# A GRU recurrence on one core: the columns of the first quarter of h are multiplied first, the rest behind them

## What is computed

```python
def cell(h, x):
    gi = x @ W_ih + b_ih
    gh = h @ W_hh + b_hh
    i_r, i_z, i_n = jnp.split(gi, 3, axis=-1)
    h_r, h_z, h_n = jnp.split(gh, 3, axis=-1)
    r = jax.nn.sigmoid(i_r + h_r)
    z = jax.nn.sigmoid(i_z + h_z)
    n = jnp.tanh(i_n + r * h_n)
    h_new = (1.0 - z) * n + z * h
    return (h_new, h_new)
xs = jnp.swapaxes(inputs, 0, 1)
_, hs = jax.lax.scan(cell, initial_state, xs)
```

## Time and profile before

| | us |
|---|---|
| median of 3 runs | 3862.88 (3861.38 to 3863.46) |
| the profiled execution | 3864.96 |
| its span in the trace | 3863.3 |
| TensorE busy in the span | 3556.0 (92%) |
| stretch 130 to 1815 us (nearly the whole recurrence): TensorE | 1616.2 of 1685.0, granted clock 1.00 |
| the same stretch: VectorE, ScalarE, GpSimd | 907.2, 851.8, 126.5 |
| the whole program: VectorE, ScalarE, GpSimd | 2105.9, 1586.6, 468.2 |

### The profile page before, as it was taken

How to read it: one execution, slowest core, us unless ns; L and a number is a source line. 1 busy time by engine, 2 the same in 40 slices (tenths; PEclk the granted TensorE clock), 3 DMA queues, 4 the chain that set the end, 5 groups by cost and what they waited for, 6 DMA issues and landing times. The chain is left out here.

```text
span 3863.3 us, 151423 instructions
## 1 busy us (share of the span) xinstructions
PE 3556.0 (92%) x60904; PEld 2248.5 (58%) x60935; DVE 2105.9 (55%) x6359; ACT 1586.6 (41%) x4769; POOL 468.2 (12%) x973
## 2 busy tenths in 40 slices
PE   5899999999999999998799999968899998999999
PEld 2578777888788878886444444424433333555554
DVE  2355555555555555554477777744466666532228
ACT  0255555555555555554344444422344444321110
POOL 1000000000000000000122222200000000024330
PEclk8999999999999999999999999979999998999999
DMA  4222222211111111111111111020111111259987
GB/s 140 87 78 77 71 71 78 66 27 25 28 26 24 27 30 27 27 27 33 57 58 38 38 57 38 19 80 22 50 57 57 57 57 40 76 177 308 295 249 295
DMA packets 220453, 298.87 MB, mean 77 GB/s; under 512 B 19955, under 2 KB 159503, under 8 KB 216416
## 3 DMA queue, kind: packets, MB, share of 16 engines
q1 hardware_dynamic: 201536, 244.94, 20.6%
q10 hardware_dynamic: 8032, 25.70, 2.3%
q0 software_dynamic: 10816, 27.33, 2.3%
HBM read 156.83 MB, written 63.96 MB: 57 GB/s over the span
## 5 line engine op out<-in xcount | busy, mean ns | idle before, releaser
L348 PE MATMUL gru_prz<-ahead,h 128*4 128x160 f32 (+1 forms) x32768 | 1179.8, 273 | 34.3 <-DVE h L459 15.1
L348 PEld LDWEIGHTS gru_prz<-ahead,h 128*4 128x4 f32 x32768 | 725.7, 87 | 201.2 <-DVE h L459 110.4
L348 PE MATMUL gru_pn<-ahead,h 128*32 128x128 f32 x16384 | 636.4, 273 | 3.5 <-issue 3.5
L348 PEld LDWEIGHTS gru_pn<-ahead,h 128*32 128x32 f32 x16384 | 509.6, 123 | 32.4 <-issue 3.8
L436 DVE STREAM_TRANSPOSE gru_tr<-gru_prz 128x160 f32<-128x160 f32 x512 | 179.0, 350 | 395.9 <-PE gru_prz L348 395.9
L410 ACT ACTIVATE gru_d<-gru_narg 128x8 f32<-128x8 f32 (+1 forms) x1024 | 209.8, 216 | 262.0 <-DVE gru_narg L447 262.0
L325 POOL COPY gru_rd<-giT 128x16 f32 x512 | 110.0, 215 | 1563.7 <-DVE h L459 1563.7
L440 DVE STREAM_TRANSPOSE gru_tn<-gru_pn 128x32 f32<-128x32 f32 (+1 forms) x1024 | 194.8, 228 | 161.2 <-PE gru_pn L348 161.2
L976 DVE TENSOR_REDUCE da_mx<-da_ps 128x2 f32<-128x1024 f32 (+3 forms) x256 | 201.1, 816 | 132.0 <-PE da_ps L669 132.0
L406 ACT ACTIVATE gru_rd<-gru_tr 128x20 f32<-128x20 f32 x512 | 122.1, 239 | 353.9 <-DVE gru_tr L436 353.9
L373 PE MATMUL gru_pgi<-gru_right,gru_left 128*128 128x128 f32 x960 | 233.8, 325 | 31.7 <-issue 29.3
(11 more groups left out here) (306 smaller groups left out, 4736.7 us busy)
## 6 DMA issues: line engine op xcount, KB each, us to landing
ahead<-in_L_ffn_gate_up_proj SPq DMA_DIRECT2D x64, 768.0 KB, 9.5
yk<-gru_zeros SPq DMA_DIRECT2D x29, 1024.0 KB, 5.0
ex_wd<-in_L_ffn_down_proj ACTq DMA_DIRECT2D x64, 384.0 KB, 8.1
ahead<-yk SPq DMA_DIRECT2D x16, 1536.0 KB, 9.6
gru_right<-ahead SPq DMA_DIRECT2D x60, 256.0 KB
gru_left<-ahead SPq DMA_DIRECT2D x60, 256.0 KB
ahead<-wide SPq DMA_DIRECT2D x15, 1024.0 KB, 4.7
ahead<-xnT SPq DMA_DIRECT2D x15, 1024.0 KB, 4.5
```

The costliest lines, as they stand in the source:

```text
L348: last = nc.tensor.matmul(rows(j), of(c), whh[:, c, j, cols], start=False, stop=True, skip_group_check=True)
```

## The change

- h's quarter 0 needs columns 0 to 31 of r, z and n. These are now multiplied first: r z0 is 64 columns (`RZ0`: r0, z0), n0 32 (`N0`), and behind them come r1 (96, `R1`), n1 (96, `N1`) and z1 (96, `Z`). A step has 5 parts instead of 3: 160 instructions on TensorE and as many loads instead of 96; the columns are the same 384 for each c and j. z's quarter 0 moves from the end of the step to its beginning, behind `h_ready[0]`.
- PSUM: one tensor `ps` of six banks, three for each copy. TensorE waits for the transpose of r z0 before n1, and for that of n0 before z1.
- VectorE has transposes for r z0 (64 columns), n0, r1 (96), n1 and z, and its order is: r z0, n0, scan of n0, r1, scan of h0, n1, scan of n1, z, scan of h1. ScalarE has a sigmoid for r z0 and one for r1, and four seeds instead of two.
- W_hh and the rows of gate inputs are laid out in the order r0 z0 r1 z1 n0 n1. W_hh comes in 80 transfers of 32 partitions with four pieces instead of 64 with three; every store of rows is two transfers.
- TensorE's loop for the last 32 steps has four steps in its body instead of two.

```diff
@@ -79,6 +79,7 @@
         block = ctx.enter_context(nc.Block())
         NBL = T // 32
         NQ = 1 + NBL
+        PIECES = ((0, 0, slice(0, 32)), (32, 1, slice(0, 32)), (64, 0, slice(32, P)), (160, 1, slice(32, P)), (256, 2, slice(0, P)))
...
-            whh = t.ahead[:].rearrange("p (c j g f) -> p c j g f", c=KD, g=3, j=KD)
+            whh = t.ahead[:].rearrange("p (c j n) -> p c j n", c=KD, j=KD)
             for jj in range(KD):
-                rows = W_hh.rearrange("(jj c i) (g j f) -> jj i c j g f", jj=KD, c=KD, g=3, j=KD)[jj]
+                rows = W_hh.rearrange("(jj c i) (g j f) -> jj i c g j f", jj=KD, c=KD, g=3, j=KD)[jj]
                 for c in range(KD):
-                    for j in range(KD):
-                        sp.dma_start(whh[32 * jj:32 * jj + 32, c, j, :, :], rows[:, c, j, :, :]).then_inc(whh_in, 16)
+                    for to, g, f in PIECES:
+                        sp.dma_start(whh[32 * jj:32 * jj + 32, c, :, to:to + f.stop - f.start], rows[:, c, g, :, f]).then_inc(whh_in, 16)
...
-                sp.dma_start(t.rows_dram[kb].rearrange("b t j f -> (b t) j f")[:, :, gate * P:(gate + 1) * P],
-                             stage[:, q % NS, :].rearrange("p (j f) -> p j f", j=KD)).then_inc(stored[q % NS], 16)
+                for to, g, f in PIECES:
+                    if g == gate:
+                        sp.dma_start(t.rows_dram[kb].rearrange("b t j f -> (b t) j f")[:, :, to:to + f.stop - f.start],
+                                     stage[:, q % NS, :].rearrange("p (j f) -> p j f", j=KD)[:, :, f]).then_inc(stored[q % NS], 16)
                 if q == 2:
-                    sp.wait_ge(stored[0], 16)
-                    sp.wait_ge(stored[1], 16)
+                    sp.wait_ge(stored[0], 32)
+                    sp.wait_ge(stored[1], 32)
...
-        RZ, Z, N = slice(0, P + 32), slice(P + 32, 2 * P), slice(2 * P, 3 * P)
+        RZ0, R1, Z, N0, N1 = slice(0, 64), slice(64, P + 32), slice(P + 32, 2 * P), slice(2 * P, 2 * P + 32), slice(2 * P + 32, 3 * P)
...
-        tr = sb("tr", [P, KD + 1, 32])
+        tr0, tr1 = sb("tr0", [P, 2, 32]), sb("tr1", [P, KD - 1, 32])
...
+        ps = ctx.enter_context(nc.psum_tensor("gru_ps", [P, 2, 3, 4 * P], F32))
...
-        R0, Z1, Z2 = 4 * P - (P + 32), 4 * P, 4 * P + P - 32
+        n1_of, rz0_of, r1_of = (lambda par: ps[:, par, 0, 256:352]), (lambda par: ps[:, par, 0, 448:512]), (lambda par: ps[:, par, 1, 0:96])
+        n0_of, z_of = (lambda par: ps[:, par, 2, 0:32]), (lambda par: ps[:, par, 2, 32:128])
+        rz_of = lambda par: ps[:, par, 0:2, :].rearrange("p k n -> p (k n)")[:, 448:608]
...
-                sp.dma_start(t.rows_dram[kb + 1].rearrange("b t j f -> (b t) j f")[:, :, 0:P],
-                             r_stage[:].rearrange("p (j f) -> p j f", j=KD)).then_inc(r_stored, 16)
+                to, of = t.rows_dram[kb + 1].rearrange("b t j f -> (b t) j f"), r_stage[:].rearrange("p (j f) -> p j f", j=KD)
+                sp.dma_start(to[:, :, 0:32], of[:, :, 0:32]).then_inc(r_stored, 16)
+                sp.dma_start(to[:, :, 64:P + 32], of[:, :, 32:P]).then_inc(r_stored, 16)
 
             def load_rows(kb, js):
-                sp.wait_ge(r_stored, 16 * (kb + 2))
+                sp.wait_ge(r_stored, 32 * (kb + 2))
                 if kb > 0:
-                    sp.wait_ge(rz_seeded, 32 * kb)
+                    sp.wait_ge(z_seeded, 32 * kb)
...
@@ -337,9 +343,9 @@
         def _(pe):
             for n in range(2):
                 for j in range(KD):
-                    nc.tensor.matmul(pn[32 * j:32 * j + 32, n, 0:P], t.ident[:, 0:32], whh[:, 0, j, N], start=True, stop=True)
-                    nc.tensor.matmul(prz[32 * j:32 * j + 32, n, R0:Z1], t.ident[:, 0:32], whh[:, 0, j, RZ], start=True, stop=True)
-                    last = nc.tensor.matmul(prz[32 * j:32 * j + 32, n, Z1:Z2], t.ident[:, 0:32], whh[:, 0, j, Z], start=True, stop=True)
+                    for k, cols in enumerate((slice(256, 512), slice(0, 96), slice(0, 128))):
+                        last = nc.tensor.matmul(ps[32 * j:32 * j + 32, n, k, cols], t.ident[:, 0:32], whh[:, 0, j, 0:cols.stop - cols.start],
+                                                start=True, stop=True)
...
-                rz_rows = lambda j: prz[32 * j:32 * j + B, par, R0:Z1]
-                n_of = lambda j: pn[32 * j:32 * j + 32, par, 0:P]
+                four = lambda of: lambda j: of(par)[32 * j:32 * j + B, :]
+                all32 = lambda of: lambda j: of(par)[32 * j:32 * j + 32, :]
                 pe.wait_ge(h_ready[0], s * 1 + 1)
                 pe.wait_ge(rz_seeded, s * 1 + 1)
-                pe.wait_ge(n_seeded, s * 1 + 1)
-                part(rz_rows, after, RZ, (0,))
-                part(n_of, places, N, (0,))
+                pe.wait_ge(z_seeded, s * 1 + 1)
+                pe.wait_ge(n0_seeded, s * 1 + 1)
+                pe.wait_ge(n1_seeded, s * 1 + 1)
+                part(four(rz0_of), after, RZ0, (0,))
+                part(all32(n0_of), places, N0, (0,))
+                part(four(r1_of), after, R1, (0,))
+                part(all32(n1_of), places, N1, (0,))
+                part(four(z_of), after, Z, (0,))
                 pe.wait_ge(h_ready[1], s * 1 + 1)
-                part(rz_rows, after, RZ, (1, 2, 3), r_rows)
-                part(n_of, places, N, (1, 2, 3), n_rows)
-                part(lambda j: prz[32 * j:32 * j + B, par, Z1:Z2], after, Z, range(KD), z_rows)
+                part(four(rz0_of), after, RZ0, (1, 2, 3), rz0_rows)
+                part(all32(n0_of), places, N0, (1, 2, 3), n_rows[0])
+                part(four(r1_of), after, R1, (1, 2, 3), r1_rows)
+                pe.wait_ge(tr0_done, s * 1 + 1)
+                part(all32(n1_of), places, N1, (1, 2, 3), n_rows[1])
+                pe.wait_ge(tn_done[0], s * 1 + 2)
+                part(four(z_of), after, Z, (1, 2, 3), z_rows)
...
-            with pe.Fori(T // 2 - 16, T // 2) as q:
-                for par in range(2):
-                    step(q * 2 + par, par)
+            with pe.Fori(T // 4 - 8, T // 4) as q:
+                for k in range(4):
+                    step(q * 4 + k, k % 2)
...
-                nc.scalar.activation(prz[:, 1 - par, R0:Z2], t.rows[:, bass.ds((s + 1) & 63, 1), :].rearrange("p o f -> p (o f)"),
-                                     ACT.Copy).then_inc(rz_seeded, 1)
-                act.wait_ge(tn_done[1], s * 1 + 1)
+                row = t.rows[:, bass.ds((s + 1) & 63, 1), :].rearrange("p o f -> p (o f)")
+                nc.scalar.activation(rz_of(1 - par), row[:, 0:P + 32], ACT.Copy).then_inc(rz_seeded, 1)
+                nc.scalar.activation(z_of(1 - par), row[:, P + 32:2 * P], ACT.Copy).then_inc(z_seeded, 1)
+                act.wait_ge(tr0_done, s * 1 + 1)
+                nc.scalar.activation(rd[:].rearrange("p (g x) -> p g x", g=2)[:, :, 0:6 * B:6], tr0[:, :, 0:B], ACT.Sigmoid).then_inc(rz0_act, 1)
                 act.wait_ge(tn_done[0], s * 1 + 1)
-                nc.scalar.activation(pn[:, 1 - par, 0:P], bias_rows[:], ACT.Copy).then_inc(n_seeded, 1)
-                act.wait_ge(tr_done, s * 1 + 1)
-                nc.scalar.activation(cb(rd[:, 0:6 * (ST + B):6]), tr[:, :, 0:B], ACT.Sigmoid).then_inc(rz_act, 1)
+                nc.scalar.activation(n0_of(1 - par), bias_rows[:, 0:32], ACT.Copy).then_inc(n0_seeded, 1)
                 for n, part in enumerate(PARTS):
                     of = slice(part.start * B, part.stop * B)
+                    if n == 1:
+                        act.wait_ge(tn_done[1], s * 1 + 1)
+                        nc.scalar.activation(n1_of(1 - par), bias_rows[:, 32:P], ACT.Copy).then_inc(n1_seeded, 1)
+                        act.wait_ge(tr1_done, s * 1 + 1)
+                        nc.scalar.activation(cb(rd[:, 6 * B:6 * ST:6]), tr1[:, :, 0:B], ACT.Sigmoid).then_inc(r1_act, 1)
...
             def step(s, par):
-                dve.wait_ge(r_rows, s * 1 + 1)
-                nc.vector.transpose(tr[:].rearrange("p c x -> p (c x)"), prz[:, par, R0:Z1]).then_inc(tr_done, 1)
-                dve.wait_ge(n_rows, s * 1 + 1)
-                for n, part in enumerate(PARTS):
-                    cols = slice(part.start * 32, part.stop * 32)
-                    nc.vector.transpose(tn[:, cols], pn[:, par, cols]).then_inc(tn_done[n], 1)
-                for n, part in enumerate(PARTS):
+                def turn_n(n):
+                    cols = slice(PARTS[n].start * 32, PARTS[n].stop * 32)
+                    dve.wait_ge(n_rows[n], s * 1 + 1)
+                    nc.vector.transpose(tn[:, cols], (n0_of, n1_of)[n](par)).then_inc(tn_done[n], 1)
+
+                def scan_n(n, r_act):
+                    part = PARTS[n]
                     of = slice(part.start * B, part.stop * B)
+                    dve.wait_ge(r_act, s * 1 + 1)
                     dve.wait_ge(tn_done[n], s * 1 + 2)
                     if n == 0:
-                        dve.wait_ge(rz_act, s * 1 + 1)
```

(21 more changed lines are left out.)

25 lines of the change are left out of this document (13 added, 12 removed).

## The result

| | before | after |
|---|---|---|
| median of 4 runs, us | 3863.17 (3861.38 to 3865.64) | 3892.25 (3889.82 to 3897.30) |
| profiled execution's span, us | 3863.3 | 3891.5 |

The ratio is 1.0079 (95% interval 1.0066 to 1.0091): slower, by 29 us. The forecast was 3874 within 3828 to 3895. The sign was right and the time in the range, but 2 us outside of the likeliest case's own range of 3862 to 3890. Only 11 of the 29 us were foreseen, and the terms behind the 11 are partly wrong in both directions.

What follows compares the result with a forecast made beforehand. TensorE was to bound 480 steps, the chain the last 32. Recurrence +1 and -2.5, opening +1.4, last loop's code +3 and stage 1 +8.1 made +11 us: median 3874, range 3828 to 3895.

Steps and rivals of the forecast that it cites:

- likeliest case: Whole kernel: n0 layers paced by the reload of their stationary, 3874 us (3862 to 3890), chance 0.52.
- TensorE becomes the bound: Main loop: TensorE needs 3.25 us a step against the chain's 3.2, so it is the bound in 480 steps.
- Turn of the loop: Every fourth main-loop step, where the inner loop turns: 0.27 us more, 3.52 us instead of 3.42 before.
- n0 bound by the reload of a strided stationary: n0's short layers: loading 32 columns of h at stride three sets their pace, 0.042 us a layer; chance 0.52.
- column-bound: Rival for the n0 layers: columns alone set 0.028 us a layer, 0.09 a step back, 3832 us; chance 0.33.
- deciding point of 0.036 a layer: n0 layers: below 0.036 us a layer the kernel was to gain.
- Chain 3.2: Transposes, scans and activations behind the columns: 3.2 us a step, bounding the last 32 steps, -2.5 us.
- Stage 1: Before the recurrence: 80 W_hh loads at 0.556 us plus 0.04 between (+4.8) and doubled stores, together +8.1 us.
- the exit: Entry into the last loop: its longer body costs one more instruction stall like the 3.54 us one, +3 us.
- Late h0: Rival: h0 comes late, needing 0.8 us past its time, and idle stays; with longer VectorE path 3895 us, chance 0.08.
- Issue: Rival: 160 matmul-load pairs a step at 0.0205 us a pair bound narrow groups, +0.55 a step, 4140 us; chance 0.04.
- Code: Rival: the main loop's 1280 loads and matmuls outgrow the engine's buffer, fetched again each pass, at least +425 us; chance 0.03.

Runs made afterwards that it cites:

- e1: Changed kernel with n0's columns multiplied with the four stationary columns of r and z instead of 32 strided ones (output not the reference's): 3863.41 us, before 3857.12.
- e2: Changed kernel with n0's 32 stationary columns taken side by side instead of every third one (output not the reference's): 3862.74 us, before 3857.12.
- e8: Kernel before with eight steps written out in TensorE's main loop instead of four: 3854.10 us, ratio 0.998, one run.
- e6: Changed kernel with r0 z0 and n0 of quarters 1 to 3 taken in turn instead of three of one, then three of the other: 3901.33 us.
- e5: Changed kernel with r0 z0 n0 merged into one group of 96 columns and all groups on the same 32 strided columns of h: 3901.52 us, ratio 1.0106.
- e9: Merged kernel (e5) with z1 instead of n1 in the PSUM bank of r0 z0 n0, the wait for their transpose moved ahead of z1: 3837.75 us, ratio 0.9944.
- e12: Merged kernel with changed banks (e9), each bank opened by one matmul per tile, z1 and r0 z0 n0 side by side: 3834.24 us, ratio 0.9936.
- e10: Merged kernel with changed banks (e9) with eight steps written out in TensorE's main loop instead of four: 4596.08 us, ratio 1.1904.

## Why the prediction was right and wrong

**TensorE becomes the bound, at 3.25: right, 0.04 short.** The mechanism is that of the trace, to the row. Idle gone in the main loop, gate input straight behind z, h0 ready before it is wanted. The sizes, foreseen and measured: quarter 0 0.67 and 0.684; r0 z0 of the others 0.33 and 0.335; n0 0.24 and 0.251; the wide groups 1.48 and 1.485; gate input 0.53 and 0.535. Every term was a little low, in proportion the n0 layer (0.042, measured 0.045) the most, and 0.04 in 3.25 is 1.2%. (The terms as printed, 2.04, 0.53 and 0.67, add up to 3.24; that of quarters 1 to 3 is 2.05.) But the sum was made against 3.28: four steps came out at 13.27 against 13.26, and measured they are 13.42, which is 0.16 x 120 = 19 us. This is the first mis-sized term, and the largest: where a forecast is a difference of two nearly equal sums, an error of one in a hundred is the whole answer.

**Turn of the loop: right.** 3.52 foreseen, 3.55 measured. Half of the turn's cost had lain in TensorE's idle time, and it came out when that was filled.

**n0 bound by the reload of a strided stationary: right, shown by e1 and e2.** The rival "column-bound" had its condition right (28 ns a layer) and its price wrong: e1 and e2 are that case, and they give 3.235 and a time 6 us above before in one run each, not 31 below it as in 3832. The sum had taken each layer's gain as the step's, and the four tiles drifting apart took half. The deciding point of 0.036 a layer falls with it.

**Chain 3.2, in the last loop only: right** (3.19; -2.4 us for -2.5).

**Stage 1: +8.1 foreseen, -1.3 measured.** The step that failed is the price of a W_hh load. I took 0.556 from the sixteen loads of the initial state, the same queue and stage; the loads with four pieces took 0.432 in the median, the other end of the bound, 0.434. So they took 39.7 us instead of 47.7, which is -3.2 and not +4.8. Both rows were of four pieces for each of 32 partitions, but the initial state is gathered value by value, and the later stage's pieces are runs of columns, as those of W_hh are. The nearer row was the one with the same kind of piece, not the one at the same place; that the piece is the reason was not tested. The doubled stores cost 1.2 at the row loads (1.7 foreseen; they start at 75.66 instead of 77.71) and 0.3 until the second idle stretch ends (1 foreseen), and TensorE's wait before the opening is 0.6 longer (0.6 foreseen for the last store). With 0.2 us of small differences this gives -1.3. In the six other runs with this stage 1 the first step starts 0.8 to 3.0 us later than in the changed kernel's trace, so the -1.3 itself is uncertain by that much.

**First pass: missing from the sum**, +5.2. Before, there was no stall in it; with 320 loads and matmuls a step instead of 192 the engine stopped once in each step. That it used up its code faster than the next of it came is my reading; no run changed that alone, but e8, with twice the steps and 192 a step, has no such stall either. I had looked for this only at the exit, where it was +4.6 for +3. The slower clock there was in neither sum.

**The rivals.** Late h0: no; but e6 shows that it needs only 0.1 us, not the 0.8 that I gave it, when the delay meets r0 z0 itself and so h1. Issue: no, e1 has 7 ns a pair. Code: no at 4 x 320 loads and matmuls, yes at 8 x 256. Where the Trainium skill ("Runtime: NRT & Kernel Launch", section "Instruction fetch mechanics") gives room for 2048 instructions, the runs agree: 8 x 192 and what else the body holds stay, 8 x 256 and the rest don't.

So the errors of stage 1 (-9.4) and of the main loop and first pass (+18 and +5) worked against one another, and the range held the result by 3 us. That the time came out in the range is luck, and so in good part is the sign: 8.1 of the 11 us by which I had the kernel slower were stage 1's, which came out no slower, and the main loop, which makes it slower, stood in the sum with +1. What was foreseen rightly is that TensorE becomes the bound, and that the reload makes the n0 layers slow.

## What to carry to other kernels

The idle time of the bounding engine isn't the gain of filling it: first take off what already lies in it (here the gate input, 0.42 of 0.54 us, and half of the loop's turn). A column group that is split to start earlier pays in the reload of its stationary; group what is needed first under one stationary instead, and where a bank's next writer has to wait for its reader, keep them apart by more than one group (e5 and e9: 0.135 us a step). And when a body is unrolled or split, count its loads and matmuls: at the first pass and the exit it costs some us, and beyond the buffer it costs every pass. Price a stall of several us at more than its length: behind it TensorE may run at half the clock.

## What the runs showed of the hardware

- A load of 32 stationary columns at a stride of three sets a pace of 45 ns for four tiles (after); 32 columns side by side give 32 ns (e2), four columns 29 ns (e1). Under layers of 82 ns or more none of them shows.
- After a run of six layers of 29 ns the four tiles start up to 58 ns apart instead of 22 (e1), after six of 32 ns up to 45 (e2), and they stay so to the end of the step.
- Behind a wait on TensorE the second layer came 122 ns after the first, not 82, where the stationary was 32 strided columns (e5, e9, e12). With four columns it was 3 to 4 ns late (140 for 136 before, 59 for 56 after).
- TensorE's granted clock fell to 0.5 during or just behind idle stretches of 3.54 us (before), 6.11 and 2.17 us (after) and 3.70 us (e10), and stayed there for some us while the engine was busy again. After the stalls of about 1 us in the first pass of after it stayed at 1.00.
- Loops of 8 steps with 192 loads and matmuls each and of 4 with 320 ran without fetching again (44 and 46 packets of instructions); 8 with 256 and 8 with 320 did not (639 and 760).
- Two openings (start set) in one PSUM bank and tile, of different columns: in e9 and e10 the output was off by the same 0.024, in e12, with one opening over both, it was not. That the second opening makes the next matmuls on the first one's columns overwrite instead of add is my reading of it, and not isolated: e12 also moved one of the parts within the bank, and e5, with two openings in one bank too, has the reference's output. By this reading e5 would have lost only n1's bias in two steps; whether that is too little to be seen is open.
